# Moving a gather's join and a router's second choice to other slots of a hand-ordered attention pipeline

## The reference

```python
x = x + tanh(g_xattn[2]) * L2_xattn(layernorm(x), ctx, ctx, mask)   # 16 heads of 8, sequence 64
x = x + tanh(g_ffn[2])   * L2_ffn(layernorm(x))
x = x + tanh(g_xattn[3]) * L3_xattn(layernorm(x), ctx, padding)     # 16 heads of 8, then LN, FFN, LN
x = x + tanh(g_ffn[3])   * L3_ffn(layernorm(x))

def L2_ffn(x):                       # 8 experts, the best 2 of each token
    xn = (x - mean(x)) * rsqrt(var(x) + eps) * gamma + beta
    probs = softmax(xn @ router_w.T / 1.5)
    w, idx = top_k(probs, 2)
    y_e = silu(xn @ W1[e]) @ W2[e]
    return x + sum over the 2 picks of w * y_e
```

## Time and profile before

| | us |
|---|---|
| three runs: median (lowest to highest) | 3188.12 (3187.03 to 3208.42) |
| the profiled execution | 3178.37 |
| its span, first to last instruction | 3176.5 |
| TensorE busy in the span | 2474.4 (78%) |
| VectorE busy | 1975.1 (62%) |
| ScalarE busy | 1354.7 (43%) |
| GpSimd busy | 1203.5 (38%) |
| mean granted TensorE clock, share of full | 0.873 |

### The profile page before, as it was taken

One profiled execution on the slowest core, in us unless ns is written; L12 is line 12 of the kernel. 1 busy time (PEld: TensorE's weight loads), 2 busy tenths in 40 slices (PEclk: granted clock), 3 DMA queues, 4 the chain that ended last, 5 costly groups with the idle time before them and its releaser, 6 DMA issues. The chain is left out here.

```text
span 3176.5 us, 63854 instructions
## 1 busy us (share of the span) xinstructions
PE 2474.4 (78%) x21496; PEld 1957.2 (62%) x21496; DVE 1975.1 (62%) x6380; ACT 1354.7 (43%) x2285; POOL 1203.5 (38%) x1253
## 2 busy tenths in 40 slices
PE   3588798588699999999688787179956877887766
PEld 0355544278577888777466565179953555566755
DVE  6588678777577666777488776220024666574578
ACT  1366300032366666566375553034323544453332
POOL 2355223211245555544212444623324444434711
PEclk9988799877899999999799987589976878887988
DMA  4300001221000000000200000122221110100001
GB/s 142 131 15 21 30 27 43 96 73 57 8 1 1 0 0 1 1 1 1 76 15 20 31 26 24 42 59 73 70 63 34 28 30 24 30 9 10 4 23 33
DMA packets 125750, 108.95 MB, mean 34 GB/s; under 512 B 15388, under 2 KB 105654, under 8 KB 124600
## 3 DMA queue, kind: packets, MB, share of 16 engines
q1 hardware_dynamic: 106552, 80.51, 8.2%
q0 software_dynamic: 8192, 16.79, 1.8%
q10 hardware_dynamic: 10752, 8.39, 0.8%
HBM read 70.52 MB, written 35.13 MB: 33 GB/s over the span
## 5 line engine op out<-in xcount | busy, mean ns | idle before, releaser
L1346 POOL TENSOR_TENSOR l1ffn_hid<-l1ffn_act 128x512 f32<-128x512 f32 x256 | 330.8, 1295 | 340.2 <-ACT l1ffn_act L1487 310.4
L1628 DVE SCALAR_TENSOR_TENSOR l1ffn_acc<-bank,l1ffn_w,l1ffn_acc 128x128 f32<-128x128 f32 x960 | 269.2, 342 | 150.1 <-PE bank L1431 142.8
L1431 PEld LDWEIGHTS bank<-l_w_ahead,l1ffn_hid 128*128 128x128 f32 x2048 | 264.8, 191 | 67.7 <-issue 49.0
L1431 PE MATMUL bank<-l_w_ahead,l1ffn_hid 128*128 128x128 f32 x2048 | 271.7, 276 | 36.8 <-DVE l1ffn_acc L1628 36.4
L1484 ACT ACTIVATE l1ffn_act<-scores,l1ffn_b 128x512 f32<-128x512 f32 x256 | 176.3, 689 | 202.3 <-PE scores L214 202.2
L2259 ACT ACTIVATE l_probs_t<-bank 128x512 f32<-128x512 f32 x256 | 141.5, 596 | 138.9 <-PE bank L229 122.4
L2327 DVE TENSOR_REDUCE l_top<-scores 128x16 f32<-128x1024 f32 x128 | 155.2, 1213 | 73.2 <-PE scores L2158 57.2
L2187 PE MATMUL bank<-l_v_blocks,l_probs_t 128*64 128x18 f32 x4096 | 157.6, 221 | 23.4 <-issue 22.2
L2704 DVE COPY l2ffn_y<-bank 128x512 f32<-128x512 f32 x34 | 23.5, 692 | 243.0 <-PE bank L2609 243.0
L212 PE MATMUL scores<-l1ffn_z_high,l1ffn_w_high 128*128 128x512 f32 x384 | 173.5, 452 | 0.0
L2187 PEld LDWEIGHTS bank<-l_v_blocks,l_probs_t 128*64 128x64 f32 x4096 | 146.9, 151 | 39.5 <-issue 36.9
(11 more groups left out here) (436 smaller groups left out, 6329.7 us busy)
## 6 DMA issues: line engine op xcount, KB each, us to landing
l2ffn_xs<-scratch_l_in SPq DMA_DIRECT2D x136, 64.0 KB, 1.8
scratch_l_out<-l2ffn_y SPq DMA_DIRECT2D x34, 256.0 KB, 2.3
x_all<-scratch_x SPq DMA_DIRECT2D x32, 256.0 KB, 3.6
l_ctx_t<-in_ctx_t SPq DMA_DIRECT2D x32, 256.0 KB
l_w_ahead<-in_l_w SPq DMA_DIRECT2D x3, 2048.0 KB, 11.7
x_all<-in_x SPq DMA_DIRECT2D x16, 256.0 KB, 3.0
l0mix_ctx<-in_ctx SPq DMA_DIRECT2D x16, 256.0 KB, 3.2
scratch_x<-l0mix_x_out ACTq DMA_DIRECT2D x16, 256.0 KB, 2.3
```

What stands on the lines that cost most here:

```text
L1346: pool.tensor_tensor(hid[:, e % K], act1[:, e % K], act3[:, e % K], ALU.mult)\
L1431: mm = pe.matmul(bank[5 + k][:, t * D:(t + 1) * D], hid[:, e % K, t * P:(t + 1) * P], w2[:, e, :], start=True, stop=True)
L1628: mm = v.scalar_tensor_tensor(out=acc[:, t, :], in0=y, scalar=w[:, h, t, e:e + 1], in1=before, op0=ALU.mult, op1=ALU.add)
```

## The change

In layer 3 the join leaves the statistics: it is made for group i + 3 in slot 3, after that slot's normalization, and the gathers run four groups ahead. The wait for the end of the join stays with the statistics (ready). Before the slots, groups 0, 1 and 2 are joined, the last of them ahead of the first shift, and four groups are gathered. In layer 2 choose_second moves from slot 3 of group 2c + 5 to slot 1 of group 2c + 6, and the last three steps of place_chosen (21 to 23, the weights) become weigh_chosen in slot 1 of group 2c + 7. No instruction is added or removed.

```diff
@@ class Gathered
-        v.wait_ge(self.joined, (i + 1) * K * G)
+
+    def ready(self, v, i):
+        v.wait_ge(self.joined, (i + 1) * self.picks.K * G)
@@ class AsItIs
+    def ready(self, v, i):
+        pass
@@ class PickTwo, vector
         if odd == 0 and 0 <= c < self.CHUNKS:
             if s == 2:
                 self.choose_first(v, c)
-            if s == 3:
+        c, odd = divmod(i - 6, 2)
+        if 0 <= c < self.CHUNKS:
+            if s == 1 and odd == 0:
                 self.choose_second(v, c)
-        c, odd = divmod(i - 6, 2)
-        if s == 3 and odd == 0 and 0 <= c < self.CHUNKS:
-            self.place_chosen(v, c)
+            if s == 3 and odd == 0:
+                self.place_chosen(v, c)
+            if s == 1 and odd == 1:
+                self.weigh_chosen(v, c)
@@ class PickTwo, place_chosen
         v.sem_inc(self.routed, 1)
+
+    def weigh_chosen(self, v, c):
...
         self.step(v, c, 21, v.tensor_tensor(taken[:, :, :, :], hot[:, :, :, :], twice(prob), ALU.mult))
@@ cross_attention, gpsimd
                 def slot(n, i, s):
-                    group(i + 3, gather, s)
+                    group(i + 4, gather, s)
...
-                for i in range(3):
+                for i in range(4):
@@ cross_attention, vector
                 def stats(i):
-                    joined.vector(v, i)
+                    joined.ready(v, i)
                     ln.vector_stats(v, i, lambda t: x_all[:, i * G + t, :])
...
                     if s == 3:
                         group(i, normalize, 0)
+                        group(i + 3, lambda g: joined.vector(v, g))
                     route.vector(v, i, s)
                     tile(n + 1, shift)
-                stats(0)
-                apply(0)
-                stats(1)
-                apply(1)
+                for i in range(2):
+                    joined.vector(v, i)
+                    stats(i)
+                    apply(i)
+                joined.vector(v, 2)
                 shift(0)
```

More of the change, by code:

```diff
@@ L1978, in place_chosen @@
         v.sem_inc(self.routed, 1)
+    def weigh_chosen(self, v, c):
+        T, E, K, picks, at = self.T, L2_E, self.picks.K, self.picks, self.chunk(c)
+        twice = lambda ap: ap[:, :, :].unsqueeze(1).to_broadcast([P, K, T, E])
+        taken, hot, weight, rsum, prob = self.taken, self.hot, self.weight, self.rsum, self.prob
         self.step(v, c, 21, v.tensor_tensor(taken[:, :, :, :], hot[:, :, :, :], twice(prob), ALU.mult))
```

## The result

The changed kernel takes 3111.51 us (median of 4, 3108.07 to 3117.04), the one before in the same comparison 3189.94 (3187.03 to 3208.42): ratio 0.9744, 95% interval 0.9704 to 0.9784. Run again later on another chip the ratio was 0.978 (0.9737 to 0.9823).

What follows compares the result with a forecast made beforehand. No engine full: a TensorE-VectorE ping-pong (scores, softmax shift) sets the pace, with clock falls. -18 - 20 - 9 + 8 + 5 = -34 from 3178.4 gives 3144, 3154 us on the median's scale; range 3122 to 3191.

Steps and rivals of the forecast that it cites:

- the clock: Layer 3, TensorE: with less idling, one of two low-clock stretches goes in every second group, 6 x 3.3 = 20 us gained.
- clock holds: Rival, chance 0.22: in layer 3 nearly all low-clock stretches go, a group takes some 25 us; 61 us gained, 3127 us.
- my two terms: Layer 3's groups: 18 us gained by moving the join and 20 us by fewer low-clock stretches.
- Layer 3, the join moved: Join from slot 1 to slot 3 of the group before: 1.5 us per group, 12 x 1.5 = 18 us gained.
- slower: Rival, chance 0.08: layer 3's clock falls behind both waits for a shift, one low stretch more per group; 41 us lost, 3229 us.
- my 3.3 us per fall: Layer 3: the time taken as the cost of one stretch of TensorE at its lower clock, 3.3 us.
- The gathers and the new wait on GpSimd: Layer 3, slot 0: the first gather's new wait for the join fits into GpSimd's wait for statistics, costing nothing.
- The end: Layer 3's last groups: gathers end a group earlier, so two groups with a join get shorter, 9 us gained.
- The start: Layer 3 before its slots: group 2's join precedes the first shift, which moves by 8.1 us; 8 us lost.
- Layer 2: Second choice and weights moved between slots: the work cancels, the clock costs 1 us per even group, 5 us lost.

Runs made afterwards that it cites:

- after_gated: The changed kernel, GpSimd holding the gathers of slots 1 and 3 until the L2200 completion that VectorE awaits is signalled: 3077.57 us, ratio 0.9665.
- before_gated: The kernel before, gathers split three, three, two over slots 0, 1, 3, first and last held until the awaited L2187 completion is signalled: 3101.48 us, ratio 0.9722.
- before_sp_rows: The kernel before with layer 3's rows of groups 3 to 15 fetched by SyncE's plain DMAs from fixed places: 3104.37 us, ratio 0.9711.
- three_buffers: The changed kernel with three group buffers for gathered rows instead of two, so gathers needn't wait for the join just before: 3128.5 us, ratio 0.9841.
- l2_only: The kernel before with only layer 2's new slots for the second choice and the weights: 3173.17 us, ratio 0.9983.
- l3_only: The changed kernel with layer 2's second choice and weights back in their old slots: 3121.46 us, ratio 0.9817 to the kernel before.

## Why the prediction was wrong

A group of layer 3 from the rows above and the earlier trace rows (the held gathers in slot 1's column also stand three, three and two to a slot):

```text
us a group                     join in slot 1   join in slot 3   the move is worth
GpSimd's gathers as written        30.2             23.5               6.7
the same, held (gated)             23.8             22.0               1.8
no indirect DMAs in the slots      23.9             21.8               2.1
```

**The step that failed: "the clock", and under it the reading of 4.83 us of idling as the join's.** I charged what I could explain of the difference between groups with and without gathers to the falls of the clock, and the falls to the join. I had the clue in hand (as an argument against the rival "clock holds": the last groups, which run almost wholly at 2.4 GHz, have no gathers) and did not ask what a gather does to TensorE. The runs show that 6.3 of the 30.2 us were the gathers' (30.2 - 23.9): 1.92 and 1.37 us of late signals in the group of the earlier trace rows; the other 3.0 I put down to the falls behind the waits that they lengthen (two low stretches a group with gathers, one without), which no run shows by itself. I sized the saving at 1.5 + 1.7 us a group; it was 5.6 (groups 1 to 11 take 328.4 us before and 266.3 after, 62.1 less; a steady one 6.7). This is the 24 us that the profiled pair has beyond the 38 of my two terms.

**Layer 3, the join moved: right in mechanism, low in size.** 1.5 us forecast, 2.1 measured with the indirect DMAs out and 1.8 with them held. Of the remaining waits I forecast 2.6 us ahead of slot 2's scores and 0.7 ahead of slot 0's; they are 1.32 and 2.29. The second is past the 2 us from which the rival "slower" was to decide, and a fall does stand behind it, yet nothing was lost: the fall of slot 2 had gone. A period of 26 to 29 us was forecast, 23.5 found.

**The clock.** It rose as forecast, to 0.91. One low stretch a group is left instead of two, in nearly every group and not in every second, and group 10, which has none, takes 23.2 us, hardly less than those with one (23.2 to 24.0). In the kernels with held gathers a low stretch costs more: groups of after_gated take 21.3 to 21.4 us without one and 22.8 to 23.0 with one, those of before_gated 22.9 and 24.2 to 24.5. So a fall goes with a loss of nothing to 1.5 us, and my 3.3 us per fall was, I take it, the price of a late signal and a fall together.

**The rival "clock holds"** (3127 us) was the nearest. The Trainium skill's section that it leaned on (TensorE: Matmul & The Clock Gate, HAM oscillation — how this bites in real kernels) ties cold bursts to long waits between them. The runs agree with the direction: with 1.32 us in place of the 4.83 the second fall went, though one still stands behind the 2.29. Of the 4.83 us the late signal made some 1.3 and the join some 2.2 (4.83 before, 3.53 in before_sp_rows, 1.32 in the changed kernel). That its time came near is in part luck: it priced the falls, and the gain was in good part late signals.

**The gathers and the new wait on GpSimd: right, at nothing.** Taking it away (three_buffers) gained nothing in the steady groups and lost in the first (37.4 us for group 0 in place of 31.8) and in groups 2 and 5 (28.7 and 28.6 in place of 25.9 and 23.2). I did not see that the wait can help, by breaking a row. **The end:** 9 us forecast; groups 12 to 14 took 28.1, 23.4, 18.5 us and take 21.8, 20.8, 18.4, so 8.9. **The start:** 8 us lost forecast; from TensorE's first transposes to group 1's first shift it is 53.3 us before and 61.1 after, so 7.7. The reason is only half mine: the shift moved by the join, and the next one because a score recorded at 2423.33 was signalled at 2433.36, 3.3 us after the last of the row of gathers:

```profile
2422.17 1.16 PE L2171 MATMUL scores<-l_k_heads,l_q_t 32*64 32x256 f32 x16
...
2429.09 0.94 POOL L1658 DMA_INDIRECT l_gathered<-scratch_l_out,l_slot  x1 [0.30 <-issue]
...
2433.38 1.23 DVE L2340 TENSOR_REDUCE l_top<-scores 128x16 f32<-128x1024 f32 x1 [12.23 <-remote]
```

**Layer 2: the sign was wrong.** I forecast 5 us lost. In the profiled pair its first to last shift takes 392.4 and 395.3 us, which seems to agree. Over all profiles it doesn't: nine with the old slots take 392.4 to 403.8 us, mean 399.5; nine with the new take 380.2 to 395.3, mean 385.5. That is 14 us gained, just outside l2_only's timed interval (13 gained to 2 lost); l3_only's time points to some 20. It is a gain by all three, but its size stays open. The odd groups 7 to 13 fall from 26.4 to 23.5 us on the mean, the even ones 8 to 14 stay at 31.2. I had charged the second choice in slot 1 of even groups in full, though the wait of VectorE in slot 3 of the same group (5.34 us for L2200 in the changed kernel) has room for it. The profiled pair is off that mean in layer 2 by 14 + 2.9 = 17 us, as much as lies between its 61 us and the medians' 78. That this is the reason is likely and not shown, since the other executions of the pair have no profile. An estimate for typical executions, with the 14: 62 + 9 - 8 + 14 = 77.

## What to carry to other kernels

When an engine is "released late by nothing visible" (the releaser is "remote", or the matmul that it waits for ended in the record 1 us or more ago), look at what GpSimd issues beside it before moving work around. With indirect DMAs in the loop, decide by a wait when they may run: behind the completion that another engine is waiting for, in short rows, or under work that the waiting engine has anyway. And compare a stretch over several profiles before believing a difference of a few us in one pair.

## What was not expected of the hardware

- While GpSimd issues indirect DMAs (0.94 us each with 0.30 us between), TensorE's semaphore updates come late: 52 of 68 with a gather beside them in the kernel before, 3 of 239 without; 1 to 2 us for a pair, 10.0 us at the start of layer 3 in the changed kernel, released up to 3.3 us after the row's end. In the places that I looked at, VectorE went on meanwhile.
- SyncE's fetches of the same size and pace, and GpSimd's own plain ones (some 560 ns each), do nothing of the kind: 23.9 us a group, with 35 GB/s as with 13.
- What in the chip is shared is open. The record's matmul ends are modelled, so whether the matmuls stall or only their signals can't be told from it; no run tried to tell it. Layer 2's scatters, also indirect, stand beside late completions too (1.58 us at 1878.17 in the changed kernel); holding them back wasn't tried.
